# Group statistics moved to the second attention's stage, half of the output moved behind block 6's turn, and both ends reordered, in a conv-attention hybrid on one core

## The chip, the core and the metric

The kernel runs on one NeuronCore of a Trainium2 chip. The metric is the device time of one launch in microseconds (us). Its engines are TensorE (PE, matrix products and transposes through them), VectorE (DVE), ScalarE (ACT), GpSimd (POOL) and SyncE (SP), which here only issues transfers. They run side by side and meet at semaphores: an instruction waits until a counter has reached a number.

## What is computed

For each of 16 images `x` of 256 channels and 32 x 32 = 1024 positions, in float32:

```python
xn = group_norm(x, 8 groups) * norm_w + norm_b
q, k, v = split(qkv_w @ xn + qkv_b)
x = x + proj_w @ (softmax(q.T @ k / 16) applied to v) + proj_b
t = tokens(x)                                # 1024 x 256
u = layer_norm(t)
n = u / |u|
t = t + softmax((n @ n.T) ** 2) @ u          # second attention
y = layer_norm(t) @ (sign(w - mean(w)) * mean(|w|)) + bias
t = t + round(clip(y, -1, 1) * 7) / 7
out = image(t)
```

## The kernel before

**Splitting for accuracy.** Products run in a rounded form of float32. Each operand is kept as a high part (rounded) and a low part (the rest), and each product is made of three: high with high, high with low, low with high. ACT mostly makes the high parts, DVE and POOL the low ones.

**Blocks and stages.** An image ("batch" `b`) is 8 blocks of 128 positions. `front(b, f, more)` of every engine is the first attention and the scores of the second, `back(b)` the rest of the second. `f` is the batch before, whose last layer (`ffn`), turn (`turn_t`) and `output` are worked in among `front(b)`. `more` is true where a next batch exists. `front(0, None, True)` comes first, then loops over `back(b-1); front(b, b-1, True)`, then the last front with `more` false, and the end for the last batch, written out with a placement `LAST` of its own in PSUM. All orders are written out by hand, one list per engine; there is no scheduler.

**The first attention's stage.** PE makes the queries (`queries`, with the query and key weights multiplied together once), the values, and for each block `n` the scores (`scores1`, L540). DVE takes the row maximum (`row_max`, L1134), ACT the exponential (`exp1`, L823), DVE turns it within 32 x 32 squares (`e1_turn`, L1143), SP sends it to `e_scratch` in memory (`send`, L383) and fetches it turned (`fetch`, L393), ACT makes the high part (`e1T_hi`, L830), DVE the low part (`e1T_lo`, L1148), and PE the product with the values (`product1`, L559 to L561). Blocks 0 to 6 go this way; the last is turned on PE (`turn_last_e1`, L586). The two halves of `e_back` and of `e_turned` are used in turn, so SP's fetch of block `n` waits for the low part of block `n - 2`, and its order is send 0, fetch 0, send 1, fetch 1 and so on. DVE adds the residual (`residual1`, with the layer norm's sums); POOL makes the scales (`layer_norm1`, `lengths`, ending in L1483), ACT the normed rows (L844), their high part (`value_rows`) and the rows of unit length (`unit_rows`, `cos_x`, L860). PE turns these (`turn_cos`, L599), ACT and DVE split them (`cosT_hi` L872, `cosT_lo` L1177).

**The second attention's stage.** `scores2` gives each block's row up to the diagonal (block 7 in two halves: parts 7 and 8), ACT squares and exponentiates (`square2` L887, `exp2` L894), DVE casts the high part (`e2_hi`, L1183) and turns it (`e2_turn`, L1198), POOL subtracts the low part (`e2_lo`, L1497), and the part above the diagonal comes back turned through memory (`send2`, `fetch2`, `e2T_hi` L900, `e2T_lo` L1206). `product2` (L629 to L631) multiplies by the normed rows. The first such products wait for the turned blocks 1 and 2.

**The next batch's group statistics.** Inside `front(b)`, DVE sums both halves of the channels (`gn_sums`, L1097 and L1099), PE spreads means over the groups (`group_means`, L508), DVE takes the deviation of each channel mean (`gn_deviation`, four steps, L1104 to L1110), PE spreads again (`group_vars`, L513), DVE adds epsilon (`gn_variance`, L1114), POOL makes scale and shift (`gn_coefficients`, L1436 to L1442), and ACT normalises in `back(b)` (`normalise`, L799). Before, the first sum stood at the head of DVE's `front`, the second behind `value_lo` 3, the deviation behind `row_max` 3, the variance behind `row_max` 4. The two spreads share the bank `narrow[1]` with values, products and turns.

**The two ends.** At the start `prepare` turns `proj_w`, multiplies the weights, and DVE, ACT and POOL split them; `signs` compares the last layer's weights with their mean. At the end PE turns the normed rows itself (`turn_ln2`, L671), and `ffn`, `clip` (L1250), `quantise` and `output` follow half by half.

Of the kernel before, what the change touches and what calls it, by code (L numbers as in the profile page):

```python
# [35 lines left out]
P = 128  # L36
# [10 lines left out]
def build(nc, x, norm_w, norm_b, qkv_w, qkv_b, proj_w, proj_b, ffn_w, ffn_b, out):  # L47
# [29 lines left out]
    with ExitStack() as ctx:  # L77
# [124 lines left out]
        qkv_loaded = sem("qkv_loaded")  # L202
        norm_loaded = sem("norm_loaded")
# [88 lines left out]
        QKV_LOADS, NORM_LOADS, FFN_LOADS = 16 * 3, 16 * 2, 16 * 3  # L292
# [51 lines left out]
        def _(sp):  # L344
# [15 lines left out]
            with nc.allow_non_contiguous_dma("columns of biases, once"):  # L360
                sp.dma_start(qkv_ld, qkv_w.rearrange("(t p) c -> p t c", p=P)).then_inc(qkv_loaded, 16)
                sp.dma_start(proj_ld, proj_w.rearrange("(t p) c -> p t c", p=P)).then_inc(qkv_loaded, 16)
                sp.dma_start(qkv_b_c[:, :], qkv_b.rearrange("(k p) -> p k", p=P)).then_inc(qkv_loaded, 16)
                sp.dma_start(norm_w_c[:, :], norm_w.rearrange("(k p) -> p k", p=P)).then_inc(norm_loaded, 16)
                sp.dma_start(norm_b_c[:, :], norm_b.rearrange("(k p) -> p k", p=P)).then_inc(norm_loaded, 16)
                sp.dma_start(ffn_ld, ffn_w.rearrange("(t p) c -> p t c", p=P)).then_inc(ffn_loaded, 16)
# [94 lines left out]
        def _(pe):  # L461
# [6 lines left out]

            def prepare():
                pe.wait_ge(qkv_loaded, QKV_LOADS)  # L470
# [6 lines left out]
                for k in range(KC):  # L477
                    for o in range(KC):
                        pe.matmul(wide[0][:, k * C:(k + 1) * C], qkv_ld[:, o, tile(k)], qkv_ld[:, KC + o, :],
                                  start=o == 0, stop=o == KC - 1)  # L480
                pe.wait_ge(gn_var, 1)
                for k in range(KC):
# [12 lines left out]
                pe.wait_ge(prep_dve, 2)  # L495
# [5 lines left out]
                pe.wait_ge(prep_dve, 3)  # L501
                pe.wait_ge(prep_act, 2)
                pe.wait_ge(prep_dve, 4)
# [188 lines left out]
            def front(b, f, more):  # L692
# [5 lines left out]
                if f is None:  # L698
                    pe.wait_ge(prep_dve, 8)
                queries(b, 1)  # L700
                if f is None:
                    pe.wait_ge(prep_dve, 12)
# [12 lines left out]
                if more:  # L715
                    pe.wait_ge(v_made, 4 * b + 4)
                    group_means(b + 1)
# [4 lines left out]
                if more:  # L722
                    group_vars(b + 1)
# [8 lines left out]
                if more:  # L732
                    pe.wait_ge(gn_var, b + 2)
# [23 lines left out]
                scores2(b, 6)  # L757
                scores2(b, 7)
                scores2(b, 8)

            def back(b):

                products2_end(b)
                for n in range(2, NT):
                    product2(b, n)
# [3 lines left out]
            group_vars(0)  # L769
            prepare()  # L770
            pe.wait_ge(prep_dve, 6)
# [22 lines left out]
        def _(act):  # L794
# [130 lines left out]
            def front(b, f, more, reuse=True):  # L925
# [89 lines left out]
            for k in range(KC):  # L1015
# [4 lines left out]
            act.wait_ge(prep_dve, 4)  # L1020
# [22 lines left out]
        def _(dve):  # L1043
# [9 lines left out]
            def prepare():  # L1053
# [4 lines left out]
                dve.wait_ge(qkv_loaded, QKV_LOADS)  # L1058
# [4 lines left out]
                dve.wait_ge(ffn_loaded, FFN_LOADS)  # L1063
                dve.tensor_reduce(w_sum[:, 0:1], ffn_ld, AX.XY, ALU.add).then_inc(prep_dve, 1)
                first_norm_lo(0)
                dve.wait_ge(prep_pe, 2)
# [529 lines left out]
```

## Time and profile before

| | |
|---|---|
| median of 3 runs | 1703.02 us (1702.33 to 1707.27) |
| the profiled execution, its own time | 1704.85 us |
| its span in the profile | 1703.1 us |
| granted TensorE clock, mean | 0.994 of full speed |
| busy share of the span | PE 97%, DVE 81%, ACT 58%, POOL 42% |

The span is the time from the first to the last instruction. Busy shares of PE count a product as busy until its modelled end, so neighbouring products overlap and short gaps vanish in them; gaps are better read from starts. In a timeline a row has start, duration, engine, line, operation, output and inputs, shape and a count of merged instructions; in brackets, where it stands, the idle time before and what ended it.

### The profile page before, as it was taken

To read this page: it belongs to the slowest core of one execution; us is meant where nothing else is said; L and a number is where in the kernel's file an instruction comes from. 1 tells how busy PE (TensorE), PEld (TensorE's weight loads), DVE (VectorE), ACT (ScalarE), POOL (GpSimd) and SP (SyncE) were. 2 spreads that over 40 slices of the span, in tenths; PEclk is the share of its full clock that TensorE was granted. 3 is DMA by queue.
4 is the path that set the end of the run, shared out by engine and by line. 5 is a ranking of instruction groups with operands and counts; after the bars stand their busy time and mean duration, and the time that the engine had idled before them with its cause. 6 is when DMAs were issued, how large, how long until landed. Compare 5 with 4: busy or idle time off the path is not lost.

```text
span 1703.1 us, 33336 instructions
## 1 busy us (share of the span) xinstructions
PE 1652.5 (97%) x10994; PEld 1511.6 (89%) x10994; DVE 1381.0 (81%) x2687; ACT 989.0 (58%) x1586; POOL 717.7 (42%) x1078
## 2 busy tenths in 40 slices
PE   7899999999999999999999999999999999999996
PEld 6798899989899898998989999898998989989895
DVE  7779688787878879788797887878788797887875
ACT  3565655657555565655657566565655656556562
POOL 1262534625345253543625346253542635336251
PEclk9999999999999999999999999999999999999998
DMA  4545546355454554545455463554545545564541
GB/s 144 154 121 170 147 152 184 124 172 158 150 165 143 172 156 151 156 152 185 135 160 161 149 184 124 175 160 146 166 149 174 161 137 155 156 186 107 173 131 56
DMA packets 218750, 259.86 MB, mean 153 GB/s; under 512 B 30176, under 2 KB 188256, under 8 KB 218720
## 3 DMA queue, kind: packets, MB, share of 16 engines
q1 hardware_dynamic: 218720, 259.48, 51.1%
q8 instruction: 17, 0.28, 0.1%
q14 instruction: 13, 0.11, 0.0%
HBM read 138.81 MB, written 120.59 MB: 152 GB/s over the span
## 4 chain that ended last, share of the span: by engine, by line
PE 36%; issue 25%; POOL 15%; DVE 13%; ACT 6%; DMA 2%; SPq 1%; POOLq 1%; DVEq 0%; ACTq 0%
PE wide L466 13%; DVE neg_max L1134 4%; POOL root_pair L1470 3%; PE turn L629 3%; PE turn L631 3%; PE turn L630 3%; PE narrow L629 3%; PE narrow L631 3%; PE narrow L630 3%; PE narrow L466 3%; DVE prob L1206 2%; POOL val L1489 2%; DMA e_scratch<-x_norm 1%; ACT expo L887 1%; DVE x_norm L1143 1%
## 5 line engine op out<-in xcount | busy, mean ns | idle before, releaser
L466 PE MATMUL wide<-xn_hi,prob 128*128 128x512 f32 x1024 | 296.0, 395 | 1.8 <-ACT expo L823 1.1
L823 ACT ACTIVATE expo<-wide,neg_max 128x1024 f32<-128x1024 f32 x128 | 142.9, 1116 | 234.2 <-DVE neg_max L1134 234.2
L466 PEld LDWEIGHTS wide<-xn_hi,prob 128*128 128x128 f32 x1024 | 187.6, 188 | 43.0 <-ACT expo L823 1.2
L1143 DVE STREAM_TRANSPOSE x_norm<-expo 128x1024 f32<-128x1024 f32 x112 | 139.4, 1244 | 51.2 <-ACT expo L823 48.7
L830 ACT ACTIVATE prob<-e_back 128x1024 fp32r<-128x1024 f32 x112 | 118.2, 1055 | 81.1 <-DMA e_back<-e_scratch 80.7
L1513 POOL TENSOR_TENSOR carrier_p<-ones 128x1 f32<-128x1 f32 x60 | 11.7, 195 | 363.5 <-DVE y_sb L1250 361.0
L1497 POOL TENSOR_TENSOR prob<-expo,prob 128x128 fp32r<-128x128 f32 (+6 forms) x112 | 146.7, 1321 | 36.0 <-DVE prob L1183 36.0
L466 PE MATMUL wide<-xn_lo,prob 128*128 128x512 f32 x512 | 160.7, 394 | 0.0
L1134 DVE TENSOR_REDUCE neg_max<-wide 128x1 f32<-128x1024 f32 x128 | 154.3, 1206 | 6.3 <-PE wide L466 6.2
L559 PE MATMUL wide<-prob 128*128 128x256 f32 x512 | 150.3, 294 | 9.0 <-DVE prob L1148 9.0
L1148 DVE TENSOR_TENSOR prob<-e_back,prob 128x1024 fp32r<-128x1024 f32 x112 | 136.0, 1214 | 20.8 <-ACT prob L830 20.3
L629 PE MATMUL turn<-val,prob 128*128 128x258 f32 x512 | 147.6, 288 | 5.0 <-DVE prob L1206 5.0
L559 PE MATMUL narrow<-prob 128*128 128x256 f32 x512 | 147.4, 288 | 1.3 <-DVE prob L1148 1.3
L561 PE MATMUL wide<-prob 128*128 128x256 f32 x512 | 146.2, 286 | 0.0
L560 PE MATMUL wide<-prob 128*128 128x256 f32 x512 | 146.1, 285 | 0.0
L631 PE MATMUL turn<-val,prob 128*128 128x258 f32 x512 | 145.5, 284 | 0.0
L630 PE MATMUL turn<-val,prob 128*128 128x256 f32 x512 | 145.3, 284 | 0.0
L629 PE MATMUL narrow<-val,prob 128*128 128x258 f32 x512 | 145.2, 284 | 0.0
L631 PE MATMUL narrow<-val,prob 128*128 128x258 f32 x512 | 144.9, 283 | 0.0
L560 PE MATMUL narrow<-prob 128*128 128x256 f32 x512 | 144.7, 283 | 0.0
L561 PE MATMUL narrow<-prob 128*128 128x256 f32 x512 | 144.7, 283 | 0.0
L630 PE MATMUL narrow<-val,prob 128*128 128x256 f32 x512 | 144.6, 282 | 0.0
(183 smaller groups left out, 5143.2 us busy)
## 6 DMA issues: line engine op xcount, KB each, us to landing
e_scratch<-x_norm SPq DMA_DIRECT2D x112, 512.0 KB, 3.6
e_back<-e_scratch SPq DMA_DIRECT2D x448, 128.0 KB, 3.0
x_raw<-in_x SPq DMA_DIRECT2D x32, 512.0 KB, 3.7
e_back<-in_x SPq DMA_DIRECT2D x64, 256.0 KB, 5.0
out<-y_sb SPq DMA_DIRECT2D x64, 256.0 KB, 3.1
ln_scratch<-x_norm SPq DMA_DIRECT2D x30, 512.0 KB, 3.0
expo<-ln_scratch SPq DMA_DIRECT2D x120, 128.0 KB, 2.9
e_scratch<-x_norm SPq DMA_DIRECT2D x32, 448.0 KB, 2.6
```

Of the source, the lines that this page charges most:

```text
L466: mm = pe.matmul(o, lhsT, r, start=first and i == 0, stop=last and i == len(parts) - 1)
L559: pe.matmul(o[:, 0:w], hi, value_hi(j), start=j == 0, stop=False)
L560: pe.matmul(o[:, 0:C], hi, value_lo(j), start=False, stop=False, skip_group_check=True)
L561: mm = pe.matmul(o[:, 0:w], lo, value_hi(j), start=False, stop=j == NT - 1)
L629: pe.matmul(o[:, 0:w], hi, val[:, j, 0:w], start=j == first, stop=False)
L630: pe.matmul(o[:, 0:C], hi, val[:, j, w:w + C], start=False, stop=False, skip_group_check=True)
L631: mm = pe.matmul(o[:, 0:w], lo, val[:, j, 0:w], start=False, stop=j == last)
L823: act.activation(expo[:, n % DEEP], wide[n % 2][:, :], ACT.Exp, bias=neg_max[:, n:n + 1], accum_out=row_sum1[:, n:n + 1]).then_inc(e1_made, 1)
L1134: dve.tensor_reduce(neg_max[:, n:n + 1], wide[n % 2][:, :], AX.X, ALU.max, negate=True).then_inc(max_made, 1)
L1143: dve.transpose(e_turned[:, n % 2].rearrange("p (q n t) -> p n q t", q=SQ, n=NT), expo[:, n % DEEP].rearrange("p (n q t) -> p n q t", q=SQ ...
L1148: dve.tensor_sub(eT_lo[n].rearrange("p (n i t) -> p n i t", n=NT, i=SQ), e_back[:, n % 2].rearrange("p i (n t) -> p n i t", n=NT), eT_hi[n ...
L1497: pool.tensor_sub(prob[:, 1, J, row], expo[:, J % DEEP, row], prob[:, 0, J, row].bitcast(F32)).then_inc(p_made, 1)
```

## The change

It renames and splits some semaphores and moves calls; no arithmetic of the result changes. On PE:

```diff
+            def query_weights(k):
+                pe.wait_ge(qkv_loaded, 16)
+                for o in range(KC):
+                    mm = pe.matmul(wide[0][:, k * C:(k + 1) * C], qkv_ld[:, o, tile(k)], qkv_ld[:, KC + o, :], ...)
+                if k == KC - 1:
+                    mm.then_inc(prep_pe, 1)
             def prepare():
-                pe.wait_ge(qkv_loaded, QKV_LOADS)
+                pe.wait_ge(proj_loaded, 16)
...
+            def weight_sums():
+                pe.wait_ge(prep_dve, 9)
                 pe.wait_ge(prep_act, 2)
                 pe.matmul(narrow[1][:, 8:10], ones[:, :], w_sum[:, :], start=True, stop=True).then_inc(prep_pe, 1)
...
                 scores1(b, 3)
-                if more:
-                    pe.wait_ge(v_made, 4 * b + 4)
-                    group_means(b + 1)
...
                 scores1(b, 4)
-                if more:
-                    group_vars(b + 1)
...
-                if more:
-                    pe.wait_ge(gn_var, b + 2)
                 product1(b, 1)
...
                 scores2(b, 6)
+                if more:
+                    group_means(b + 1)
                 scores2(b, 7)
                 scores2(b, 8)
+                if more:
+                    group_vars(b + 1)
             def back(b):
                 products2_end(b)
                 for n in range(2, NT):
+                    if n == 3:
+                        pe.wait_ge(gn_var, b + 2)
                     product2(b, n)
...
+            for k in range(KC):
+                query_weights(k)
             prepare()
...
-            for n in range(2, NT - 2):
+            for n in range(2, NT - 1):
                 product2(f, n)
             pe.wait_ge(sq2_made, NP * f + NP)
             turn_ln2(f, 0, LAST)
-            product2(f, NT - 2)
             product2(f, NT - 1)
             ffn(f, 0, LAST)
+            turn_ln2(f, 1, LAST)
             turn_t(f, 0, LAST)
-            turn_ln2(f, 1, LAST)
             ffn(f, 1, LAST)
```

On SP the loads at the start go in the order x, `qkv_w`, `norm_w`, `norm_b`, `proj_w`, `qkv_b`, then the rest, and `proj_w` and `qkv_b` have semaphores of their own. On ACT:

```diff
                 act.wait_ge(len_steps, 3 * (N1 * b + g + 1))
+                act.wait_ge(ln1_made, NT * b + n1)
...
                 layer_norm1(b, 3)
+                unit_rows(b, 3)
                 square2(b, 3)
                 exp2(b, 3)
-                unit_rows(b, 3)
...
-            act.wait_ge(prep_pe, 1)
+            normalise(0, 0, False)
+            act.wait_ge(prep_pe, 2)
             act.activation(projT, turn[:, 0:KC * C]..., ACT.Copy).then_inc(prep_act, 1)
-            for k in range(KC):
-                normalise(0, k, False)
-                norm_hi(0, k, False)
+            norm_hi(0, 0, False)
+            normalise(0, 1, False)
+            norm_hi(0, 1, False)
```

On DVE (in `prepare` the split of the query weights comes first and the sum of the last layer's weights last; `signs` is cut in two, and its comparisons go from the head of the first front to the second attention's stage):

```diff
                 if f is None:
...
-                    signs()
-                if more:
-                    gn_sums(b + 1, 0)
+                    weight_means()
                 query_lo(b, 0)
...
                 value_lo(b, 3)
-                if more:
-                    gn_sums(b + 1, 1)
...
                 row_max(b, 3)
-                if more:
-                    gn_deviation(b + 1)
                 e1T_lo(b, 0)
...
                 row_max(b, 4)
-                if more:
-                    gn_variance(b + 1)
...
                 residual1(b, 1)
-                if f is not None:
-                    output(f, 1)
                 row_max(b, 6)
                 e1T_lo(b, 3)
                 e1_turn(b, 6)
+                if f is not None:
+                    output(f, 1)
                 row_max(b, 7)
...
                 cosT_lo(b, 1)
+                if more:
+                    gn_sums(b + 1, 0)
                 residual1(b, 7)
                 cosT_lo(b, 2)
+                if f is None:
+                    signs()
                 e2_turn(b, 1)
+                if more:
+                    gn_sums(b + 1, 1)
                 e2_hi(b, 2)
...
                 e2_turn(b, 5)
+                if more:
+                    gn_deviation(b + 1)
                 e2_hi(b, 6)
                 e2_turn(b, 6)
+                if more:
+                    gn_variance(b + 1)
                 e2T_lo(b, 1)
...
-            residual2(f, 4)
-            residual2(f, 5)
+            for n in range(HT, NT - 1):
+                residual2(f, n)
             ln2T_lo_last(f, 0, LAST)
-            for n in range(NT - 2, NT):
-                residual2(f, n)
+            residual2(f, NT - 1)
             clip(f, 0)
+            quantise(f, 0)
             ln2T_lo_last(f, 1, LAST)
-            quantise(f, 0)
             output(f, 0, LAST)
```

On POOL `gn_coefficients(b + 1)` goes from behind `quantise(f, 1)` to the end of `front`, behind `e2_lo(b, 6)`.

## Rows read from the trace of the kernel before

**Rows 1.** The waits of PE: who waited for whom, us in total, times, longest us.

```profile
PE wide L559 <- DVE prob L1148: 9.0, 13, 3.1
PE narrow L599 <- ACT cos_x L860: 8.7, 16, 0.6
PE turn L629 <- DVE prob L1206: 5.0, 16, 0.4
```

**Rows 2.** Timeline of PE: the queries and block 6's first product, batches 14 and 15.

```profile
1470.55 0.62 PE L466 MATMUL wide<-xn_hi,qk_lo 128*128 128x512 f32 x2
...
1530.72 0.39 PE L559 MATMUL wide<-prob 128*128 128x256 f32 x1 [0.44 <-DVE prob L1148]
...
1573.87 0.62 PE L466 MATMUL wide<-xn_hi,qk_lo 128*128 128x512 f32 x2
...
1632.89 0.34 PE L559 MATMUL wide<-prob 128*128 128x256 f32 x1
```

**Rows 3.** Timelines of SP (block 6's fetches, batches 14 and 15) and DVE (batch 15).

```profile
1523.84 1.73 SPq L393 DMA_DIRECT2D e_back<-e_scratch  x4
...
1625.83 1.73 SPq L393 DMA_DIRECT2D e_back<-e_scratch  x4
...
1621.78 1.23 DVE L1134 TENSOR_REDUCE neg_max<-wide 128x1 f32<-128x1024 f32 x1 [0.44 <-PE wide L466]
1622.92 1.22 DVE L1148 TENSOR_TENSOR prob<-e_back,prob 128x1024 fp32r<-128x1024 f32 x1
```

**Rows 4.** Timelines of POOL, ACT and DVE around the last unit rows, batch 14.

```profile
1540.91 0.70 POOL L1483 TENSOR_TENSOR len_i<-len_e,minus_one 128x2 f32<-128x2 f32 x1
...
1541.27 0.58 ACT L887 ACTIVATE expo<-wide 128x512 f32<-128x512 f32 x1
...
1542.42 0.90 ACT L860 ACTIVATE cos_x<-ln_x,len_i 128x256 f32<-128x256 f32 x2
...
1545.19 0.69 DVE L1177 TENSOR_TENSOR tokT_lo<-narrow,tokT_hi 128x512 fp32r<-128x512 f32 x1 [1.65 <-ACT tokT_hi L872]
```

**Rows 5.** Timelines of POOL and DVE where their operations meet, batch 14.

```profile
1549.59 1.86 POOL L1497 TENSOR_TENSOR prob<-expo,prob 128x768 fp32r<-128x768 f32 x1 [0.49 <-DVE prob L1183]
1552.01 2.13 POOL L1497 TENSOR_TENSOR prob<-expo,prob 128x896 fp32r<-128x896 f32 x1 [0.56 <-DVE prob L1183]
...
1506.01 1.06 POOL L1440 TENSOR_TENSOR gn_ma<-gn_m,gn_a 128x2 f32<-128x2 f32 x1
...
1498.56 0.16 DVE L1106 TENSOR_TENSOR gn_d<-gn_mv,gn_m 128x2 f32<-128x2 f32 x1
...
1550.71 1.22 DVE L1183 CAST prob<-expo 128x896 fp32r<-128x896 f32 x1 [0.45 <-ACT expo L894]
...
1552.74 1.87 DVE L1206 TENSOR_TENSOR prob<-x_tok,prob 128x128 fp32r<-128x128 f32 x2
```

**Rows 6.** Timelines of PE and DVE at the start; last, the first turn of batch 14.

```profile
10.21 3.46 PE L479 MATMUL wide<-tok 128*128 128x256 f32 x8
...
17.55 0.70 PE L466 MATMUL wide<-xn_hi,qk_lo 128*128 128x512 f32 x2 [0.28 <-DVE xn_lo L1051]
...
34.01 1.25 DVE L1143 STREAM_TRANSPOSE x_norm<-expo 128x1024 f32<-128x1024 f32 x1 [1.27 <-ACT expo L823]
...
1484.53 1.25 DVE L1143 STREAM_TRANSPOSE x_norm<-expo 128x1024 f32<-128x1024 f32 x1 [0.17 <-ACT expo L823]
```

**Rows 7.** Timelines of PE and DVE at the end.

```profile
1674.54 1.06 PE L671 MATMUL wide<-ident,ln 128*128 128x128 f32 x8 [4.14 <-ACT ln L865]
...
1690.30 0.79 PE L680 MATMUL narrow<-tokT_lo,sign_w 128*128 128x512 f32 x1 [2.41 <-DVE tokT_lo L1245]
...
1682.89 0.17 DVE L1214 RECIPROCAL inv_sum<-narrow 128x1 f32<-128x1 f32 x1 [1.50 <-PE narrow L631]
```

**Rows 8.** Stretches: length, busy PE, PEld, DVE, ACT, POOL, granted clock, DMA share, GB/s.

```profile
1676.00:1680.00 4.00, 4.00 (x24) 4.00 (x24) 1.22 (x1) 1.15 (x2) 0.00 (x0) 0.62 0.00 0
1686.00:1688.00 2.00, 1.09 (x8) 0.85 (x8) 0.00 (x0) 2.00 (x5) 0.00 (x0) 1.00 0.00 0
```

More of the change, by code:

```diff
@@ L202, in build @@
         qkv_loaded = sem("qkv_loaded")
+        proj_loaded = sem("proj_loaded")
+        qkv_b_loaded = sem("qkv_b_loaded")
         norm_loaded = sem("norm_loaded")
@@ L290, in build @@
         stored = [sem("stored0"), sem("stored1")]
-        QKV_LOADS, NORM_LOADS, FFN_LOADS = 16 * 3, 16 * 2, 16 * 3
+        NORM_LOADS, FFN_LOADS = 16 * 2, 16 * 3
         block = ctx.enter_context(nc.Block())
@@ L467, in three @@
                 return mm
+            def query_weights(k):
+                pe.wait_ge(qkv_loaded, 16)
+                for o in range(KC):
+                    mm = pe.matmul(wide[0][:, k * C:(k + 1) * C], qkv_ld[:, o, tile(k)], qkv_ld[:, KC + o, :],
+                                   start=o == 0, stop=o == KC - 1)
+                if k == KC - 1:
+                    mm.then_inc(prep_pe, 1)
             def prepare():
-                pe.wait_ge(qkv_loaded, QKV_LOADS)
+                pe.wait_ge(proj_loaded, 16)
                 for j in range(KC):
@@ L475, in prepare @@
                 mm.then_inc(prep_pe, 1)
-                for k in range(KC):
-                    for o in range(KC):
-                        pe.matmul(wide[0][:, k * C:(k + 1) * C], qkv_ld[:, o, tile(k)], qkv_ld[:, KC + o, :],
-                                  start=o == 0, stop=o == KC - 1)
                 pe.wait_ge(gn_var, 1)
+                pe.wait_ge(qkv_b_loaded, 16)
                 for k in range(KC):
@@ L493, in prepare @@
                 mm.then_inc(prep_pe, 1)
-                pe.wait_ge(prep_dve, 2)
+                pe.wait_ge(prep_dve, 4)
                 for o in range(KC):
@@ L698, in front @@
                 if f is None:
-                    pe.wait_ge(prep_dve, 8)
+                    weight_sums()
                 queries(b, 1)
                 if f is None:
-                    pe.wait_ge(prep_dve, 12)
+                    pe.wait_ge(prep_dve, 10)
                 else:
@@ L769, in _ @@
             group_vars(0)
+            for k in range(KC):
+                query_weights(k)
             prepare()
-            pe.wait_ge(prep_dve, 6)
+            pe.wait_ge(prep_dve, 3)
             front(0, None, True)
@@ L1010, in back @@
                     layer_norm2(b, n)
-            act.wait_ge(prep_pe, 1)
+            normalise(0, 0, False)
+            act.wait_ge(prep_pe, 2)
             act.activation(projT, turn[:, 0:KC * C].rearrange("p (t c) -> p t c", c=C), ACT.Copy
                            ).then_inc(prep_act, 1)
-            for k in range(KC):
-                normalise(0, k, False)
-                norm_hi(0, k, False)
+            norm_hi(0, 0, False)
+            normalise(0, 1, False)
+            norm_hi(0, 1, False)
             act.wait_ge(ffn_loaded, FFN_LOADS)
             act.activation(abs_w, ffn_ld, ACT.Abs, accum_out=w_sum[:, 1:2]).then_inc(prep_act, 1)
-            act.wait_ge(prep_dve, 4)
+            act.wait_ge(prep_dve, 5)
             front(0, None, True)
@@ L1057, in prepare @@
                                 ).then_inc(prep_dve, 1)
-                dve.wait_ge(qkv_loaded, QKV_LOADS)
+                dve.wait_ge(prep_pe, 1)
+                g = wide[0][:, 0:KC * C].rearrange("p (k c) -> p k c", k=KC)
+                dve.tensor_scalar(qk_hi[:, :, :], g, scale, None, ALU.mult).then_inc(prep_dve, 1)
+                dve.wait_ge(prep_dve, 2)
+                dve.scalar_tensor_tensor(qk_lo[:, :, :], g, scale, qk_hi[:, :, :].bitcast(F32),
+                                         ALU.mult, ALU.subtract).then_inc(prep_dve, 1)
+                dve.wait_ge(qkv_b_loaded, 16)
                 for o in range(KC):
@@ L1528, in front @@
                     quantise(f, 1)
-                if more:
-                    gn_coefficients(b + 1)
                 layer_norm1(b, 0)
@@ L1549, in front @@
                 e2_lo(b, 6)
+                if more:
+                    gn_coefficients(b + 1)
             def back(b, more):
```

30 lines of the change are left out of this document (12 added, 18 removed).

## The prediction

> **What bounds the kernel now.** I read the page first (TensorE, PE, is nearly always busy, the other engines are not), then what PE waited for, then the PE timeline batch by batch, then the other engines around each of PE's waits. PE is the bound, so a change pays only where PE stands still. Besides the two ends it stands in three places of a batch [rows 1]: at the first attention's products of block 6 (9.0 us in 13 times; batches 0 and 1 take more than half of it, the others some 0.4 each), at the last turn of the unit rows (8.7 us, 16 times, on `cos_x`), and at the second attention's first product that needs transposed blocks (5.0 us, 16 times, on L1206). A batch takes 1573.87 - 1470.55 = 103.3 us [rows 2]. 14 further batches behave like batch 14, which I use as the pattern; batch 15 computes no next statistics, so the trace holds a batch with the statistics taken out.
>
> **The first attention's stage.** The change takes 2 x 1.4 us of sums (two BN_STATS and an aggregate, 1.28 us and the rest), four small steps of the deviation and one of the variance off VectorE (DVE), and two tiny products off PE. Batch 15 prices it: block 6's product starts 1530.72 - 1470.55 = 60.17 us after the queries in batch 14, and 1632.89 - 1573.87 = 59.02 in batch 15 [rows 2], without a wait. The reason stands on SP: the transposed blocks go out and back through memory one after the other, and block 6's fetch starts 53.3 us after the queries in batch 14 and 52.0 in batch 15 [rows 3]. 1.15 us is the most; batch 14 waits slightly longer than the mean of its like (0.44 against some 0.4, [rows 1, 2]), and the scatter of the transfers will sometimes still pass PE. I take -0.95 us a batch.
>
> **The output's second half behind block 6's turn.** It is 1.3 us on DVE and now stands ahead of `row_max` 7 and of block 4's low part. In batch 15 DVE idled 0.44 us before `row_max` 7, and the output no longer delays what came before, so these two go back by 0.67 us: the low part ends at 1622.92 + 1.22 + 0.67 = 1624.8 instead of 1624.1, and the fetch of block 6, which waits for it, starts at 1625.83 [rows 3]. It is hidden by 1.0 us. The last exponential goes back by 0.67 too and touches PE's turn of the last block by about 0.05 us. Nothing is taken.
>
> **The unit rows ahead of square 3.** This is the edit against PE's wait on `cos_x` (0.54 us each, 0.7 from start to start). ScalarE (ACT) now waits for the inverse lengths of GpSimd (POOL), which end at 1540.91 + 0.70 = 1541.61; square 3 started at 1541.27 [rows 4]. So `cos_x` starts at 1541.64 rather than 1542.42 and PE's wait goes. But ACT stands 0.37 us in a stretch where it was full, and everything behind, up to the copy of the turned rows, is 0.37 late. The low half behind it on DVE ended at 1545.19 + 0.69 = 1545.88 [rows 4], and block 6 of the second scores needs it. PE, coming 0.7 us earlier, waits for it there, and starts that block 0.37 later than now. The gain moves one product on and turns into a loss of 0.4: a chain through POOL, ACT and DVE sets this stage.
>
> **The statistics in the second attention's stage.** The first sum lies in DVE's wait for block 7's product, the second in its wait for exponential 3: nothing, or up to 0.2 us. POOL's coefficients (2.2 to 3.3 us of small steps) come after its last low part, which ends at 1554.14 [rows 5], some 5 us before ACT needs them; the two tiny products cost PE 0.3 us in front of a place where it waits anyway. The deviation is another matter. It stands between `e2_turn` 5 and the cast of block 6, and POOL computes block 5's low part from 1549.59 to 1551.45 [rows 5]. The rows show that the two engines don't run such operations together: the cast of block 6 was issued at 1550.71 and took 1.22 us, ending 0.48 after POOL's operation; the pair at L1206, 128 and 256 columns wide, took 1.87 us from 1552.74 and ended 0.47 after POOL's next one (1552.01 + 2.13); and a POOL step of two columns took 1.06 us beside a DVE subtraction, against 0.20 for its like [rows 5]. The deviation holds three operations of two SBUF inputs, 0.16 us and a gap each, 0.19 [rows 5]. The first will wait for POOL's end, so the cast starts 0.6 us behind that end and takes its 0.5 us then, instead of standing ready. With the 0.37 of the chain, POOL's next low part, and behind it L1206, and behind that PE's first crossed product, come 0.4 + 0.65 = 1.05 us later. PE reaches the place 0.7 late by then and waits the rest. Bounds: 0.4 (the deviation finds POOL's port free or slips in before), and 1.5 (it is held a second time).
> The Trainium skill, SBUF — State Buffer, Who interferes with whom, states this as a lock: a DVE instruction with two SBUF inputs contends with a GpSimd one that reads SBUF, and whichever starts first has the shared pair for its whole duration. This is what the rows show for large operations; no row has one of two columns on DVE waiting. By a lock that spared such small ones, the sum would be the first rival's.
>
> So an inner batch comes to -0.95 + 1.05 = +0.1 us, and 14 of them (1 to 14) to +1.4.
>
> **The start.** ACT's second normalisation now waits for the transposes of `proj`, and these for the query weights, 3.46 us on PE [rows 6]. I work that out to bring the queries from 17.55 to about 19. In exchange the signs and a sum no longer stand ahead of DVE's first low parts: the first turn came 34.01 - 17.55 = 16.5 us after the queries in batch 0, and 1484.53 - 1470.55 = 14.0 in a settled batch [rows 2, 6]. -2.5 + 1.4 = -1.1, and since batch 0's block 6 hangs on the chain of transfers that this turn begins, PE gets just that: -1.0 (between -2.5 and +0.5). The back of batch 0 costs the same +1.05, and the signs, two scalar comparisons and a subtraction beside POOL's small steps, 1.4 to 5 us on DVE, of which I let +1.2 through.
>
> **The end.** Batch 15 has no next statistics and pays only the 0.4 of the unit rows. PE then waited 4.14 us for the first normed rows [rows 7]; `product2` 6, 2.9 us at full speed, now lies in that wait. Behind it two products ran, partly at the lower of PE's clock levels (a granted 0.62 in those 4 us, that is 1.2 GHz for most of it, [rows 8]); now one does, after a wait of some 1.3 us. After waits of about 1.2 us in this trace the granted clock stays 1.00 (the stretch from 1686) [rows 8]. The last residual at 1682.89 [rows 7] comes 2.9 + 1.5 - 0.4 = 4.0 earlier. Of this, `quantise` 0, two operations of 0.7, gives back 1.1 ahead of the second half's low part: PE's last layer starts 2.9 to 3 us sooner than 1690.30, still at 1.2 GHz (0.79 us for a product that took 0.40 elsewhere, [rows 7]). Net of the 0.4: -3.3 for the reordering.
>
> **Sum**: start -1.0, batch 0's back +1.05 and +1.2, inner batches +1.4, batch 15 +0.4, end -3.3: -0.25 us. The profiled execution has a span of 1703.1 us and 1.75 around it; the median of the runs, 1703.02, happens to equal the span. I set 1702.7 against that median. About 0.3%, 5.1 us, is what a measurement can tell from no change.
>
> **Rivals.**
> 1. *The deviation is not held up by POOL.* Then the back costs 0.4 in place of 1.05: 15 x 0.65 = 9.8 us less, 1693 us. For it: its operations have two columns. Against it: the POOL step of two columns that took 1.06 us. 25%.
> 2. *Slower: the output's second half holds block 6's fetch.* The low part of block 4, behind the output and `row_max` 7 on DVE, releases the fetch buffer. If it ends more than the 1.0 us later, SP waits for DVE instead of for the write, and the front's 0.95 is lost in 14 batches: 1702.7 + 13.3 = 1716. It decides from 1625.8 in batch 15's terms [rows 3]. Against it: the 1.0 us. 10%.
> 3. *The clock falls in every batch*, since PE now has three shorter waits within 12 us. Each would cost some 1.5 us (a granted 0.62 over 4 us, [rows 8]), 21 us in all: 1724. All three waits lie under those that left the clock at 1.00. 5%.
>
> **How the numbers follow.** The forecast has 60%, with 1698 to 1707 as its own range (the bounds of start, signs and scatter). The whole range, 1692 to 1708, takes in the first rival and leaves out the second and third. Faster by over 0.3%: the first rival and a small part of the forecast, 0.31; slower: the second, the third and 0.01 or so, 0.15; the same: 0.54.
>
> **What the next profile would show.** Right: block 6's first product some 59.1 us after the queries and hardly a wait there; no PE wait on `cos_x` but one of about 1 us on L1177, at a `wide` product; gn_d on DVE lasting about 1 us or more; the wait on L1206 longer than 0.3; the inner batch at 103.4. If the inner batch takes 102.8 and gn_d 0.16, the first rival holds. A fetch of block 6 released by L1148 rather than by the write is the second; stretches with a granted 0.5 in the middle of batches are the third. The end should keep one wait of about 1.3 us before L671, and queries starting near 19 us with the signs far behind would confirm the start.

## The result, and the profile after

The changed kernel takes 1710.55 us (median of 10 runs, 1708.58 to 1712.34) against 1703.02 for the kernel before (10 runs, 1699.54 to 1707.27). The ratio is 1.0041, 95% interval 1.0031 to 1.0051. The change makes the kernel 7 us slower. The forecast was 1702.7 with a range up to 1708.

The profiled execution has a span of 1709.9 us. First the page's lines on busy time, and then what PE waited for in the changed kernel (columns as in [rows 1]):

```profile
PE 1646.4 (96%) x10994; PEld 1506.6 (88%) x10994; DVE 1403.5 (82%) x2687; ACT 985.7 (58%) x1586; POOL 725.3 (42%) x1078
```

```profile
PE turn L593 <- ACT expo L830: 18.7, 14, 1.3
PE wide L468 <- DVE tokT_lo L1188: 12.4, 16, 0.9
...
PE wide L566 <- DVE prob L1159: 3.4, 2, 2.9
PE narrow L636 <- issue: 3.1, 13, 0.2
PE narrow L687 <- DVE tokT_lo L1256: 2.7, 1, 2.7
PE turn L678 <- ACT ln L873: 2.1, 1, 2.1
```

PE is the bound as before, and its three waits of [rows 1] have given way to others. The one on `cos_x` is down to 0.6 us, once, and the one on the crossed product's transposed blocks (L1206, now L1217) is gone. The 12.4 us at the scores of block 6 stand in their place. The first line is new and the largest: 1.34 us in each of 14 batches, at the turn of the last block of the first attention. PE's wait for block 6 remains only in batches 0 and 1. PE's timeline of batch 13, from its queries to the next ones:

```profile
1376.54 0.62 PE L468 MATMUL wide<-xn_hi,qk_lo 128*128 128x512 f32 x2
...
1429.10 0.77 PE L593 MATMUL turn<-ident,expo 128*128 128x128 f32 x5 [1.34 <-ACT expo L830]
...
1437.16 0.28 PE L566 MATMUL wide<-prob 128*128 128x256 f32 x1
...
1452.58 0.66 PE L468 MATMUL wide<-tokT_hi,tokT_lo 128*128 128x512 f32 x2 [0.77 <-DVE tokT_lo L1188]
...
1480.75 0.62 PE L468 MATMUL wide<-xn_hi,qk_lo 128*128 128x512 f32 x2
```

A batch takes 104.2 us against 103.3 in [rows 2]. Block 6's first product comes 1437.16 - 1376.54 = 60.62 us after the queries, without a wait on it, and it comes so in every inner batch (inner batches are 2 to 14 from here on). It came at 60.17 before and 59.02 in the batch without statistics [rows 2]. Over the inner batches the mean is 60.63 after and 60.06 before, and the way from there to the next queries is 43.54 us after and 43.17 before. So the first attention's stage, which was to give 0.95 us, costs 0.57, and the rest of the batch, "the back" from here on, costs 0.37.

Now DVE, POOL and ACT in the 10 us ahead of that turn:

```profile
1419.90 1.22 DVE L1159 TENSOR_TENSOR prob<-e_back,prob 128x1024 fp32r<-128x1024 f32 x1
1424.18 1.25 DVE L1154 STREAM_TRANSPOSE x_norm<-expo 128x1024 f32<-128x1024 f32 x1 [3.06 <-ACT expo L830]
1425.35 1.25 DVE L1277 TENSOR_TENSOR y_sb<-turn,y_sb 128x512 f32<-128x512 f32 x2
1426.52 1.21 DVE L1145 TENSOR_REDUCE neg_max<-wide 128x1 f32<-128x1024 f32 x1
...
1420.32 0.85 POOL L1485 TENSOR_TENSOR ln_shift<-ln_neg,root_pair 128x2 f32<-128x2 f32 x1
...
1421.20 1.09 ACT L851 ACTIVATE ln_x<-tok,ln_shift,root_pair 128x256 f32<-128x256 f32 x2 [3.31 <-POOL ln_shift L1485]
...
1427.84 1.11 ACT L830 ACTIVATE expo<-wide,neg_max 128x1024 f32<-128x1024 f32 x1 [2.04 <-DVE neg_max L1145]
```

Read it backwards. PE's turn waits for exponential 7, which waits for `row_max` 7. That stands behind the output's second half (L1277, 1.17 us from start to start), and the output stands behind the turn of block 6, ahead of which DVE is idle for 3.06 us. Before the change the output stood ahead of that idle time. A second thing shows on POOL: its step L1485, two columns wide, takes 0.85 us beside DVE's subtraction L1159. In the kernel before this step, at 44.57 us after the queries, takes 0.20. ACT's normed rows wait for it, and exponential 6 stands behind them. The next pair's step (L1485 at 1435.79, 59.25 us after the queries) takes 0.83 beside another subtraction L1159, against 0.20 before; what that costs no run shows.

The second attention, DVE and POOL around the deviation of the same batch:

```profile
1455.76 0.23 DVE L1117 TENSOR_TENSOR gn_d<-gn_mv,gn_m 128x2 f32<-128x2 f32 x1
1456.02 1.78 DVE L1119 TENSOR_TENSOR gn_e<-gn_d 128x2 f32<-128x2 f32 x1
1457.83 0.16 DVE L1121 TENSOR_TENSOR gn_e<-gn_e,gn_mv 128x2 f32<-128x2 f32 x1
1457.93 0.63 DVE L1194 CAST prob<-expo 128x896 fp32r<-128x896 f32 x1
...
1455.94 1.84 POOL L1509 TENSOR_TENSOR prob<-expo,prob 128x768 fp32r<-128x768 f32 x1
```

The deviation is held by POOL, as forecast, and two columns are no protection. The first operation, issued 0.18 us ahead of POOL's, takes 0.23. The second, issued 0.08 us behind it, lasts until POOL's ends. The Trainium skill's lock (SBUF — State Buffer, Who interferes with whom: issue order, not shape, decides who blocks) agrees with these rows.

### The profile page after: what moved, and what is told of

Same layout as the page of the kernel before. It is cut to its first block, busy times and chain, and to the rows that moved or that the text cites. A ratio compares the mean times of both kernels' runs of the same rounds, so it can differ in the third digit from the quotient of the medians.

```text
span 1709.9 us, 33396 instructions
## 1 busy us (share of the span) xinstructions
PE 1646.4 (96%) x10994; PEld 1506.6 (88%) x10994; DVE 1403.5 (82%) x2687; ACT 985.7 (58%) x1586; POOL 725.3 (42%) x1078
## 4 chain that ended last, share of the span: by engine, by line
PE 52%; issue 23%; POOL 14%; ACT 4%; DVE 3%; DMA 2%; SPq 1%; POOLq 0%; DVEq 0%; ACTq 0%
PE wide L468 21%; PE narrow L468 5%; PE narrow L636 3%; POOL root_pair L1482 3%; PE turn L687 3%; PE turn L636 3%; PE turn L638 3%; PE turn L637 3%; PE narrow L638 3%; PE narrow L637 3%; POOL len_i L1495 2%; POOL ln_shift L1485 2%; POOL val L1501 2%; DMA e_scratch<-x_norm 2%; ACT expo L895 1%
## 5 line engine op out<-in xcount | busy, mean ns | idle before, releaser
L1477 POOL TENSOR_TENSOR var_pair<-ln_mv,eps_or_none 128x4 f32<-128x4 f32 x64 | 12.9, 202 | 352.8 <-DVE ln_mv L1182 352.8
L1159 DVE TENSOR_TENSOR prob<-e_back,prob 128x1024 fp32r<-128x1024 f32 x112 | 135.4, 1209 | 12.3 <-ACT prob L837 12.3
```

What stands on the lines that cost most here:

```text
L1159: dve.tensor_sub(eT_lo[n].rearrange("p (n i t) -> p n i t", n=NT, i=SQ), e_back[:, n % 2].rearrange("p i (n t) -> p n i t", n=NT), eT_hi[n ...
```

## The experiments

Four questions: what does the output's place cost, and by which way; what is the move of the statistics worth without it; what do the unit rows and the deviation cost; and what do the ends give. The differences below are each run's median against the kernel before, measured on the same chip at the same time (1701.60 us beside e1 to e4, 1700.84 beside e5 to e8, 1699.54 beside e9 to e11). The quoted ratios pair the runs round by round, and where two ratios put two kernels at another distance than the medians do, both are given. Times after the queries, of the back and of a batch are means of batches 2 to 14, worked out from each run's timeline.

**e1: the output's second half back in its old place**, all else as changed.

```
                 residual1(b, 1)
+                if f is not None:
+                    output(f, 1)
                 row_max(b, 6)
                 e1T_lo(b, 3)
                 e1_turn(b, 6)
-                if f is not None:
-                    output(f, 1)
                 row_max(b, 7)
```

> The changed kernel with the output's second half back behind residual1(b,1), all else as changed. Theory A (the output ahead of row_max 7 delays exponential 7 and PE's turn of the last block): the wait of 1.3 us on exponential 7 at L593 goes, the turn of the last block comes about 1.3 us sooner after the queries (52.6 -> 51.3), block 6's product 60.6 -> 59.2 to 59.6; 14 batches give 14 to 20 us: 1691 to 1697. Theory B (the front is slow for another reason, such as the loop's own batches, and the output only stands where the time shows): within 3 us of the changed kernel's 1710.6.

Measured: 1693.84 us, ratio 0.9961 (0.9947 to 0.9974): 7.8 us under the kernel before, where the changed one is 7.5 above, so 15 us apart (14 by the ratios). PE's turn of the last block comes 51.00 us after the queries (52.56 in the changed kernel) and block 6's product at 59.23 (60.63). Theory A holds, the turn coming even 0.3 us sooner than it said. The rows of e1, batch 13, queries at 1360.77:

```profile
1407.77 1.25 DVE L1154 STREAM_TRANSPOSE x_norm<-expo 128x1024 f32<-128x1024 f32 x1 [1.24 <-ACT expo L830]
1408.94 1.19 DVE L1145 TENSOR_REDUCE neg_max<-wide 128x1 f32<-128x1024 f32 x1
...
1404.56 0.20 POOL L1485 TENSOR_TENSOR ln_shift<-ln_neg,root_pair 128x2 f32<-128x2 f32 x1
...
1411.77 0.60 PE L593 MATMUL turn<-ident,expo 128*128 128x128 f32 x4
```

`row_max` 7 starts 48.17 us after the queries and not 49.98. That is 1.81 us: 1.17 for the output and 0.64 for the turn of block 6, which comes at 47.00 and not 47.64. PE can take 0.25 us of it: with the changed kernel's 2.58 us from `row_max` 7 to PE's turn, PE would be served at 50.75 and arrives at 51.00. 1.81 - 0.25 = 1.56, exactly what the turn of the last block loses.

**e2: the output one place later**, behind `row_max` 7 and ahead of block 4's low part.

```
                 row_max(b, 7)
+                if f is not None:
+                    output(f, 1)
                 e1T_lo(b, 4)
```

> The changed kernel with the output's second half one place later, behind row_max 7 and ahead of block 4's low part. Theory A1 (only the 1.27 us ahead of row_max 7 count): the wait on exponential 7 falls to near zero, block 4's low part and the fetch of block 6 stay where they are in the changed kernel: 1.0 us a batch, 1696. Theory A2 (it is as much the GpSimd step beside block 3's low part, 0.85 us instead of 0.20, that delays exponential 6 and the turned block 6): exponential 7 gains 1.3 but ends 0.65 later than in the run with the output before row_max 6; 4 to 8 us slower than that run. Rival R2 of the forecast (block 4's low part holds the fetch of block 6): no gain at all, 1710.

Measured: 1697.36 us, ratio 0.9978 (0.9969 to 0.9987). A1 and A2 both hold, A2 a little under its 4 to 8 us. Without the output ahead of it, `row_max` 7 is free of 1.17 us, but the step on POOL is still held (batch 13 of e2), and 0.64 - 0.25 = 0.39 us should be left. PE's turn of the last block comes at 51.37 and not 51.00, and 3 to 4 us against e1 are left of the loss.

```profile
1407.62 0.85 POOL L1485 TENSOR_TENSOR ln_shift<-ln_neg,root_pair 128x2 f32<-128x2 f32 x1
```

Block 6's product is at 59.62 although block 4's low part is as late as in the changed kernel, and SP's fetch of block 6 still waits for it (in batch 13 for 3.0 us). The forecast's second rival, by which this hold takes the stage's 0.95 us, would have allowed no gain at all. As the cause of the loss it falls.

**e3: the output between `row_max` 6 and block 3's low part.**

```
                 row_max(b, 6)
+                if f is not None:
+                    output(f, 1)
                 e1T_lo(b, 3)
```

> The changed kernel with the output's second half between row_max 6 and block 3's low part, so that DVE's operation with two SBUF inputs again starts after the GpSimd step. By A2 the step L1485 takes 0.2 us again and exponential 6 comes 0.65 us sooner; DVE stood idle for about 3 us between block 3's low part and the turn of block 6, so that the output is hidden there too and exponential 7 comes 1.3 + 0.65 us sooner than in the changed kernel: as the run with the output before row_max 6 within 3 us, 1690 to 1697. If block 3's low part, now 1.3 us later, holds the fetch of block 5, the time is 1700 or more.

Measured: 1693.31 us, ratio 0.9952 (0.9938 to 0.9966), not to be told from e1. L1485 takes 0.20 us again in this group of steps. So what matters is that the output stands ahead of DVE's idle time, and that DVE's subtraction with two SBUF inputs starts behind POOL's step.

**e4: the kernel before, with the output's move alone.**

```
                 residual1(b, 1)
-                if f is not None:
-                    output(f, 1)
                 row_max(b, 6)
                 e1T_lo(b, 3)
                 e1_turn(b, 6)
+                if f is not None:
+                    output(f, 1)
                 row_max(b, 7)
```

> The kernel before with nothing but the output's second half moved behind the turn of block 6. Theory A: exponential 7 comes 1.3 us later, the turn of the last block goes from 51.5 to 52.8 us after the queries, block 6's product from 60.1 to about 60.8: 14 x 0.7 = 10 us slower than before, 1713. Theory B: 1703, within 2 us.

Measured: 1720.01 us, ratio 1.0113 (1.0097 to 1.0129), 18.4 us slower than before. Theory A's direction, but nearly twice its 10 us. The waits of PE in e4:

```profile
PE turn L586 <- ACT expo L823: 18.7, 14, 1.3
PE narrow L599 <- ACT cos_x L860: 8.7, 16, 0.6
...
PE turn L629 <- DVE prob L1206: 5.1, 16, 0.4
...
PE wide L559 <- ACT expo L823: 3.3, 14, 0.3
```

PE's turn comes at 53.36 us after the queries and not 51.51, and block 6's product at 61.43 and not 60.06. I had taken 52.8. POOL's step takes 0.85 us here too, so `row_max` 7 goes from 48.96 to 50.78, by 1.82 and not by 1.3, and all of it reaches PE's turn: in the kernel before it comes 2.55 us after `row_max` 7, as close as in the changed kernel (2.58), with nothing to spare. PE also stands up to 0.3 us, 14 times, at an earlier product that waits for exponential 6, late by the same step. A batch is 104.49 us against 103.23. The same move costs 104.16 - 102.87 = 1.29 us a batch in the changed kernel and 1.26 here, so it is nearly independent of the rest.

**e5: e1 with the last unit rows back behind exponential 3.**

```
                 layer_norm1(b, 3)
-                unit_rows(b, 3)
                 square2(b, 3)
                 exp2(b, 3)
+                unit_rows(b, 3)
```

> The kernel of e1 (changed, output's second half before row_max 6) with the last unit rows back behind exponential 3. By the forecast's step the edit costs 0.4 us a batch in all, so that taking it out gives about 6 us: 1688. By the waits of PE it trades one for another: 0.54 on cos_x and 0.3 on L1206 in the kernel before against 0.76 on L1188 in e1, so nothing or 1 us a step: 1694, within 2. In the trace the wait on cos_x should be back and the one on L1188 gone or below 0.2.

Measured: 1695.58 us, ratio 0.9968 (0.9957 to 0.998); the interval overlaps that of e1. The waits of e5:

```profile
PE narrow L606 <- ACT cos_x L868: 8.6, 16, 0.8
...
PE narrow L520 <- DVE gn_e L1121: 3.6, 15, 0.8
```

The wait on `cos_x` is back, the one on L1188 gone, and PE waits 0.2 us a batch for the deviation. By the timeline, block 6's product to the next queries takes 43.85 us against 43.64 in e1. The edit gains 0.2 us a batch here. Pair e8 and e7, below, shows it the other way where the deviation isn't in this stage: 43.16 without it, 43.36 with it, a loss of 0.2. The forecast's +0.4 is too much in both.

**e6: e1 with the deviation's three operations left out for the next batch.** Only the means are copied, and all batches use the first one's variance.

```
-                    gn_deviation(b + 1)
+                    gn_mean_only(b + 1)
...
+            def gn_mean_only(b):
+                dve.wait_ge(gn_mean_up, b + 1)
+                dve.tensor_copy(gn_m[:, :], gn_up).then_inc(gn_dev, 1)
```

> The kernel of e1 with the deviation's three operations of two SBUF inputs left out for the next batch (only the means are copied; the variance of the first batch's channels serves all). By the forecast's step they cost 0.65 us a batch, 15 times: 1684. By the trace of the changed kernel the cast behind them is held by GpSimd's low part of block 5 in any case and PE no longer waits at L1206: nothing, 1694, within 2.

Measured: 1688.88 us, ratio 0.9921 (0.9908 to 0.9935), 4 us (medians) to 7 us (ratios) under e1 and between the two theories. The back takes 43.25 us against 43.64. The deviation costs 0.39 us of the back, not 0.65 and not nothing. Of a whole batch it is 0.27 (102.60 against 102.87), since block 6's product comes 0.12 later in e6, where PE more often waits for its fetch. PE at the product of the group variances, first e1, then e6:

```profile
1441.01 0.31 PE L520 MATMUL narrow<-gn_e,group_mean 128*128 128x2 f32 x2
1441.51 0.38 PE L636 MATMUL narrow<-val,prob 128*128 128x258 f32 x1 [0.20 <-issue]
```

```profile
1438.33 0.28 PE L520 MATMUL narrow<-gn_e,group_mean 128*128 128x2 f32 x2
1438.47 0.37 PE L636 MATMUL narrow<-val,prob 128*128 128x258 f32 x1
```

From start to start 0.50 us against 0.14, 0.36 us: PE's own queue stands at this product for the deviation, and the next products start late.

**e7: e1 with the statistics in the first attention's stage**, on all engines, as in the kernel before (the calls of `group_means`, `group_vars`, `gn_sums`, `gn_deviation`, `gn_variance` and `gn_coefficients` go back to their old lines).

```
+                if more:
+                    gn_sums(b + 1, 0)
                 query_lo(b, 0)
...
                 row_max(b, 3)
+                if more:
+                    gn_deviation(b + 1)
...
                 e2_turn(b, 5)
-                if more:
-                    gn_deviation(b + 1)
```

> The kernel of e1 with the statistics of the next batch back in the first attention's stage, on all engines, as in the kernel before. By block 6's product (60.1 us after the queries in the kernel before, 59.2 in e1) the move is worth 0.9 us in each of 14 batches: 1706. By the forecast's own sum the back gives 0.65 of it back: 1698. If the ends carry all of what e1 gained over the kernel before: 1694.

Measured: 1700.37 us, ratio 0.9992 (0.9981 to 1.0002), between the two numbers. Against the kernel before, e1 gained 7.8 us and e7 0.5: the move of the statistics is worth 7 us (5 by the ratios). The timeline says where: block 6's product 59.98 us after the queries in e7 and 59.23 in e1 (0.75 gained, forecast 0.95), the back 43.36 and 43.64 (0.28 given back).

**e8: the kernel before with the ends alone** (start, signs, last products).

```
-            for n in range(2, NT - 2):
+            for n in range(2, NT - 1):
                 product2(f, n)
...
             turn_ln2(f, 0, LAST)
-            product2(f, NT - 2)
             product2(f, NT - 1)
```

> The kernel before with the two ends alone changed (start, signs, last products), statistics, unit rows and output as before. The forecast's terms: start -1.0, signs +1.2, end -3.3: 3.1 us less than before. By the changed kernel's trace: start and batch 0 some -1.3, batch 15 and the end -4.0: 5.3 us less.

Measured: 1696.09 us, ratio 0.997 (0.9958 to 0.9982), 4.8 us less than before; the expectation from the changed kernel's trace said 5.3. From batch 15's queries to the end of the span 1694.2 - 1569.56 = 124.6 us, against 1703.1 - 1573.87 = 129.2 before: 4.6 us by the end. The two profiled executions lie 8.9 us apart in all (1703.1 and 1694.2), more than the medians, so this share is rough.

The next three ask whether the two waits that e1 has left can go.

**e9: the product of the variances later on PE**, nothing left out.

```
             def products2_end(b, more=True):
                 for j in range(2, NT):
+                    if more and j == 4:
+                        group_vars(b + 1)
...
                 scores2(b, 8)
-                if more:
-                    group_vars(b + 1)
...
                 e2T_lo(b, 2)
+                if more:
+                    gn_variance(b + 1)
```

> The kernel of e1 with PE's product of the group variances moved from behind the last scores (where it waits for the deviation) into the crossed products, 1.4 us later, and DVE's step that reads it behind the second low part of the transposed blocks. Left in: the deviation, held by GpSimd as before. If its price is PE's own wait at that product (in e1 the first product behind it starts 0.50 us after it, in e6 0.14), nearly all of what e6 gained comes back with nothing left out: 0.36 x 15 = 5.4 us, 1688.5. If the price is what the forecast said, the later low parts behind it: nothing, 1694.

Measured: 1692.71 us, ratio 0.9949 (0.9935 to 0.9964), 2 us under e1 by the ratios and 1 over it by the medians; the times don't tell the two apart. The gap behind the product is 0.14 us in e9,

```profile
1442.14 0.28 PE L520 MATMUL narrow<-gn_e,group_mean 128*128 128x2 f32 x2
1442.28 0.37 PE L636 MATMUL narrow<-val,prob 128*128 128x258 f32 x1
```

but the back shrinks only by 0.12 us, to 43.52. Of the deviation's 0.39 us, 0.12 is PE's wait alone. The other 0.27 returns a few products on, for DVE's low parts are late by the same hold:

```profile
1443.66 0.28 PE L638 MATMUL turn<-val,prob 128*128 128x258 f32 x1
1443.86 0.39 PE L636 MATMUL turn<-val,prob 128*128 128x258 f32 x1
1444.09 0.28 PE L637 MATMUL turn<-val,prob 128*128 128x256 f32 x1
```

From start to start these take 0.20 and 0.23 us where their neighbours take 0.12, and the first of them starts just behind the end of DVE's pair at L1217 (at 1443.81). PE's wait and the late low parts are two effects of one cause, and the forecast's step had named the second.

**e10: ACT's copy of the last turned unit rows ahead of exponential 4.**

```
                 square2(b, 4)
+                cosT_hi(b, 3)
                 exp2(b, 4)
-                cosT_hi(b, 3)
```

> The kernel of e1 with ACT's copy of the last turned unit rows ahead of exponential 4 instead of behind it: DVE's low half and with it PE's wait at the scores of block 6 (L1188, 12.2 us in 16 times) come 0.7 us sooner. If that chain alone sets the stage: 16 x 0.7 = 11 us, 1683. If exponential 4, now 0.6 us later, puts GpSimd's low parts and the crossed products behind: 1688 to 1694.

Measured: 1685.73 us, ratio 0.9911 (0.9896 to 0.9926). The wait on L1188 is gone from the list, and the back takes 43.06 us against 43.64. It is 6 us (ratios: 8) under e1, where an independent wait would have given 11. Of the 0.58, 0.08 is lost again in front of block 6's product (59.31 against 59.23), so a batch gains 0.50; why it isn't the full 0.7 no run shows. What PE waits for in e10:

```profile
PE wide L566 <- DVE prob L1159: 6.3, 8, 3.1
PE narrow L636 <- issue: 2.9, 13, 0.3
```

**e11: both edits.**

> The kernel of e1 with both edits, that of e9 and that of e10. If the two waits are independent: 5 + 11 us, 1678. If the earlier PE only runs into the deviation or into the transposed blocks (L1217): between the better of the two and that.

Measured: 1682.85 us, ratio 0.9895 (0.9879 to 0.991): 16.7 us under the kernel before and the lowest time of all, though its interval overlaps that of e10. The back takes 42.92 us and a batch 102.19. It too misses the full sum. Means of the timelines have its first crossed products 0.81 us sooner than e10's, and at the end of the back 0.14 are left. As in e9, I read this as PE catching up with the low parts; the wait on L1217 is in its list only twice, with 0.6 us.

## Why the prediction was wrong

**The step that failed** is "The output's second half behind block 6's turn ... Nothing is taken". The forecast put `row_max` 7 back by 0.67 us, took 0.44 us of DVE's idle time ahead of it, and let the last exponential touch PE's turn by 0.05 us. Measured, `row_max` 7 goes back by 1.81 us and PE's turn by 1.56, and a batch takes 1.29 more (e1 against the changed kernel; 1.26 in e4). Four things were wrong in it. (a) It let the output's absence make earlier what had stood behind it. But the turn of block 6 waits for exponential 6: DVE is idle ahead of it for 1.24 us in e1, with the output in its old place, and for 3.06 without. Taken from ahead of this wait the output gave nothing, and put behind it, it cost its whole length of 1.17 us. (b) It let 0.44 us of idle time ahead of `row_max` 7 cover a part. That row is batch 15's [rows 3]; in e1's batch 13 `row_max` 7 follows the turn at once (1407.77 and 1408.94), with nothing to cover anything, and so it does in the inner batches of the kernel before (below). Both together are 1.17 - 0.67 = 0.5 us. (c) It did not see that the vacated place moves DVE's subtraction onto POOL's step L1485, which goes from 0.20 to 0.85 us and delays ACT's normed rows, exponential 6 and so block 6's turn by 0.64 us (e2 and e3 tell it apart). The forecast applied this very lock to the deviation, one stage on, and not here. (d) It gave PE a margin of 0.67 - 0.05 = 0.62 us, and there are 0.25. The sum: 0.05 + 0.5 + 0.64 + 0.37 = 1.56.

The turn of block 6 and `row_max` 7 in batch 14 of the kernel before:

```profile
1518.33 1.25 DVE L1143 STREAM_TRANSPOSE x_norm<-expo 128x1024 f32<-128x1024 f32 x1 [1.24 <-ACT expo L823]
1519.50 1.18 DVE L1134 TENSOR_REDUCE neg_max<-wide 128x1 f32<-128x1024 f32 x1
```

In batch 15 the forecast's sizes came true: there `row_max` 7 goes from 47.91 to 48.54 us after the queries (0.63, forecast 0.67), PE's turn from 51.01 to 51.13 (0.12, forecast 0.05), and POOL's step takes 0.19. The forecast read this edit off the last batch, which isn't like the inner ones. The missing idle time and the missing margin already stood in the trace of the kernel before; the lock on POOL's step stood in no row of it and could only be expected.

**The statistics out of the front**: right, -0.95 forecast and -0.75 measured (e7 to e1). In the changed kernel it could not show, since the turn of the last block had become the bound in this stage.

**Block 6's fetch**: the forecast was wrong that it isn't held and right that PE doesn't lose by it. Block 4's low part and the fetch in batch 13 of the changed kernel,

```profile
1427.65 1.20 DVE L1159 TENSOR_TENSOR prob<-e_back,prob 128x1024 fp32r<-128x1024 f32 x1
...
1428.93 1.25 SPq L395 DMA_DIRECT2D e_back<-e_scratch  x3
```

and what SP waited for ahead of it, first there (1426 to 1430), then in e1 (batch 13, 1412 to 1417):

```profile
SPq L393 <- DVE prob L1159: 3.0, 1, 3.0
```

```profile
SPq L395 <- DMA e_scratch<-x_norm: 1.8, 1, 1.8
```

In e1 SP waits for the write of block 6, as in the kernel before; in every inner batch of the changed kernel it waits for the low part, in some for the write after it. The low part ends at 52.32 us after the queries and not at 50.48, so it goes back by 1.84 us and not by 0.67. That was the condition of the second rival, and the sign that the forecast gave for it. Its price did not come: in e1 the write lets the fetch start at 52.35, in the changed kernel it starts at 52.55, 0.20 later and not 0.95, and the products of block 6 wait for it in no inner batch. e2 has the same hold and gains 1.0 us a batch. The slower rival had the right operation, and with 1716 a time of the right side, but the wrong victim: not the transfer but the exponential behind `row_max` 7. The forecast looked only at the chain of transfers, since this had been the last wait of the stage, and dismissed the other chain in one sentence.

**The unit rows**: the mechanism was right. The wait on `cos_x` went and turned up on L1188 at a `wide` product, 0.77 us where about 1 was forecast. The price was +0.2 or -0.2 us a batch with the surroundings (e7 against e8, e1 against e5), not +0.4. The move was neither the gain it looks like nor the loss that was forecast.

**The deviation**: right in kind, too large in size. It is held by POOL, but only one operation of the three, and the cast behind it would have been held as well. It costs 0.39 us of the back in place of 0.65 (e6). The wait on L1217 that was to grow is gone: PE stands earlier, at L520. The first rival (not held, 1693) is false. With the output in place e1 comes to 1693.84 all the same, but by other terms: that is luck.

**The clock**: the third rival is false. The stretch from 100 to 1600 us of the changed kernel (columns as in [rows 8]) has a granted clock of 1.00:

```profile
100.00:1600.00 1500.00, 1467.06 (x9862) 1345.27 (x9861) 1259.11 (x2413) 882.35 (x1419) 661.76 (x961) 1.00 0.52 155
```

**Start, signs, end**: mis-sized, on the good side. Up to batch 2's queries the profiled executions give 230.56 us after and 231.91 before, -1.35 where the terms sum to some +1.35. The queries start at 18.77 us, as forecast (about 19). The end gives 129.2 - 125.2 = 4.0 us, with 2.9 forecast after the unit rows' share. PE's last layer at the end:

```profile
1698.05 0.50 PE L687 MATMUL narrow<-tokT_lo,sign_w 128*128 128x512 f32 x1 [2.68 <-DVE tokT_lo L1256]
1698.39 0.39 PE L687 MATMUL narrow<-tokT_hi,sign_w 128*128 128x512 f32 x1
...
1699.79 0.63 PE L687 MATMUL narrow<-tokT_lo,sign_w 128*128 128x512 f32 x1
```

The first takes 0.50 us, the next three 0.39 to 0.40, and from 1699.36 on they take 0.63; in [rows 7] the first took 0.79. The stretch's line (columns as in [rows 8]) has a granted clock of 0.76, so it is partly at 2.4 GHz and partly at 1.2:

```profile
1698.00:1705.00 7.00, 4.50 (x16) 3.44 (x16) 3.66 (x7) 1.45 (x2) 0.00 (x0) 0.76 0.24 75
```

The forecast had it at 1.2 GHz all through.

**The sum, against the profiled executions** (the forecast counts batch 1 with the inner ones; here it is with the start): 13 inner batches are 12.2 us longer (1.3 forecast), start and first two batches 2.7 us better than forecast, batch 15 and the end 1.1 better: 10.9 - 2.7 - 1.1 = 7.1 us from the forecast's -0.25 to the +6.8 of the spans. By the experiments an inner batch is: ends -0.1 (e8 against before, scatter), unit rows +0.2 (e7 against e8), statistics -0.47 (e1 against e7), output +1.29 (the changed kernel against e1): +0.9.

## What to carry to other kernels

Before an operation is moved along an in-order queue, look for the idle time that it passes. Here it cost nothing ahead of the wait, and behind it its length for all that followed; what comes earlier by its leaving is only what was not waiting. A vacated place can have a cost too: the next operation starts sooner, and here it then met a step on POOL, which took 0.85 us in place of 0.20. Read idle times and margins in the batches that the edit acts on 14 times, not in an odd one at the end. And when one chain's last wait goes, price the second chain of the stage with the same care, since a margin of 0.25 us was all there was here; undoing this one move turned 7 us more than before into 8 us less.

## What the hardware showed

- Very small operations are held by large ones of the other engine, on DVE and on POOL: a DVE multiplication of two columns took 1.78 us beside POOL's subtraction, and a POOL step of two columns 0.85 us beside DVE's, against 0.16 and 0.20 for their like. In the first case the operation issued 0.18 us ahead of POOL's took 0.23, and the one issued 0.08 behind it 1.78. I had expected it of the deviation; that the step on POOL would fall under it in every inner batch, as soon as the output in front of DVE's subtraction was gone, I had not.
- The queries of batch 0 start at 17.55 us in the profiled execution of the kernel before and at 19.74 in e4, which has the same start. By the queries of batch 2 they are 0.31 us apart (231.91 and 231.60). A gain or loss of a microsecond at the first queries can't be read from one profile.
